# Waiting for freed ring slots in front of every fourth gather, for two groups at once, instead of every second

## The reference

```python
h = relu(layernorm(x))
H = gelu(h @ W1.T + b1)                        # [6250, 128]
X_src = H[src]                                 # [200000, 128]: a gather by edge
W_tar = gelu(X_src @ WA.T) @ WB.T              # [200000, 4]
cross = X_src[:, :, None] * W_tar[:, None, :]
agg = gelu(segment_sum(cross, dst))            # [6250, 128, 4]
out_edge = einsum('ehm,em->eh', agg[dst], W_tar)
agg_node = segment_sum(out_edge, dst) / max(count(dst), 1)
out = x + gelu(concat([agg_node, H])) @ W2.T + b2
```

## Time and profile before

| | |
|---|---|
| median of three runs | 1236.04 us |
| the profiled execution | 1235.48 us |
| its span in the trace | 1233.7 us |
| TensorE (PE) matmul busy | 1053.0 us, 85% |
| VectorE (DVE) busy | 901.9 us, 73% |
| GpSimd (POOL) busy | 851.9 us, 69% |
| ScalarE (ACT) busy | 634.3 us, 51% |
| gathers (L780) | 796, 780.5 us busy |

### The profile page before, as it was taken

The page is one execution under the profiler, slowest core; times in us unless marked ns, Lnnn a source line. Parts: engine busy times, 40 slices in busy tenths (PEclk is TensorE's granted clock), DMA queues, the critical chain, the costliest instruction groups (busy, mean ns, idle before and its releaser), DMA issues.

```text
span 1233.7 us, 26415 instructions
## 1 busy us (share of the span) xinstructions
PE 1053.0 (85%) x7416; PEld 743.9 (60%) x7416; DVE 901.9 (73%) x2876; ACT 634.3 (51%) x1498; POOL 851.9 (69%) x910
## 2 busy tenths in 40 slices
PE   4957776658999998999799899889899989779987
PEld 3744333337778766677576676667676765446644
DVE  8648998884888687898487888668788866263275
ACT  6977766535455465676276667456566540000033
POOL 5437775555777777777777777777777777767445
PEclk9975666668999999999899999989899999889979
DMA  6335554447777755565655556555555667866632
GB/s 217 127 118 177 182 176 158 154 141 218 203 204 213 203 160 155 155 171 166 177 161 160 162 153 169 160 157 165 145 161 161 163 195 213 189 184 186 196 25 88
DMA packets 100422, 205.73 MB, mean 167 GB/s; under 512 B 29570, under 2 KB 48336, under 8 KB 99611
## 3 DMA queue, kind: packets, MB, share of 16 engines
q1 hardware_dynamic: 74804, 146.92, 40.0%
q0 software_dynamic: 25472, 57.11, 18.8%
HBM read 171.73 MB, written 32.22 MB: 165 GB/s over the span
## 4 chain that ended last, share of the span: by engine, by line
PE 42%; DVE 16%; POOL 13%; issue 12%; DMA 8%; ACT 5%; DVEq 3%; SPq 0%; ACTq 0%; POOLq 0%
PE ps L1581 20%; POOL q L780 13%; PE ps L1528 10%; PE ps L1547 7%; DMA q<-node_table,src_g 6%; DVE big L1338 3%; DVE big L1197 3%; PE ps L1531 2%; DVE q L1206 2%; DVE big L1184 2%; DVE mask L1172 2%; PE ps L1586 2%; DVEq L1154 2%; ACT big L823 1%; DMA out_dram<-q 1%
## 5 line engine op out<-in xcount | busy, mean ns | idle before, releaser
L780 POOL DMA_INDIRECT q<-node_table,src_g x796 | 780.5, 981 | 294.6 <-issue 214.4
L1581 PE MATMUL ps<-big,q 128*128 128x298 bf16 (+2 forms) x2940 | 528.9, 301 | 8.2 <-DMA q<-product_parts 7.6
L896 ACT ACTIVATE hot_b<-iota_b,q 128x128 bf16<-128x128 bf16 x848 | 270.0, 389 | 245.4 <-PE ps L1547 245.1
L1528 PE MATMUL ps<-mask,q 128*128 128x96 f32 x1592 | 275.2, 300 | 93.5 <-DVE mask L1172 90.3
L1581 PEld LDWEIGHTS ps<-big,q 128*128 128x128 bf16 x2940 | 267.9, 99 | 110.1 <-DMA q<-product_parts 7.7
L1528 PEld LDWEIGHTS ps<-mask,q 128*128 128x128 f32 x1592 | 236.3, 209 | 147.1 <-DVE mask L1172 133.4
L1206 DVE TENSOR_SCALAR q<-iota_a,q 128x294 bf16<-128x294 f16 (+2 forms) x848 | 238.1, 324 | 38.2 <-issue 22.8
L1547 PE MATMUL ps<-q,hot_b 128*128 128x294 bf16 (+2 forms) x848 | 211.2, 334 | 45.1 <-DVE big L1197 37.6
L1197 DVE TENSOR_TENSOR big<-big,ps 128x294 f32 (+2 forms) x411 | 225.9, 550 | 19.5 <-PE ps L1547 17.9
L1172 DVE TENSOR_TENSOR mask<-eq,q 128x192 f32<-128x192 bf16 x398 | 141.2, 356 | 121.6 <-DMA q<-node_table,src_g 106.0
L1184 DVE TENSOR_TENSOR big<-big,ps 128x120 f32 x398 | 110.1, 277 | 81.1 <-DVE big L1184 42.3
(11 more groups left out here) (145 smaller groups left out, 658.9 us busy)
## 6 DMA issues: line engine op xcount, KB each, us to landing
q<-product_parts SPq DMA_DIRECT2D x245, 388.0 KB
product_parts<-big SPq DMA_DIRECT2D x24, 776.0 KB, 3.5
q<-node_table,src_g POOLq DMA_INDIRECT x796
node_table<-big SPq DMA_DIRECT2D x12, 280.0 KB, 3.1
big<-node_table SPq DMA_DIRECT2D x24, 140.0 KB, 2.2
own_part<-big SPq DMA_DIRECT2D x12, 256.0 KB, 3.2
out_dram<-q SPq DMA_DIRECT2D x12, 256.0 KB, 2.0
big<-own_part SPq DMA_DIRECT2D x2, 1024.0 KB, 6.5
```

The costliest lines, as they stand in the source:

```text
L780: pool.indirect_dma_start(out=ring[:, t % R, :], out_offset=None, in_=table, in_offset=bass.IndirectOffsetOnAxis(ap=src_g[:, t:t + 1], axi ...
L896: last = nc.scalar.activation(hot_b[:, b % 2, i, :], iota_b[:, :], ACT.Abs, bias=nkey_b[:, t:t + 1])
L1528: nc.tensor.matmul(o[:, 0:MIX * W], ring[:, s + t, 0:D], mask[:, b, t, :, :], start=(t == 0), stop=(t == G - 1))
L1581: last = nc.tensor.matmul(ps[:, 3 + m, 0:n], cb[:, LEAD + P * (MIX * part + m):LEAD + P * (MIX * part + m + 1)], counts[k % 2][:, a, c0:c1 ...
```

## The change

```diff
             for t in range(TG):
                 if t == 2:
                     pool.memset(c3[:, :, :, 0:LEAD], 0.0).then_inc(lead_zeroed, 1)
-                if t >= R and t % G == 0:
-                    pool.wait_ge(group_summed, (t - R) // G + 1)
+                if t >= R and t % (2 * G) == 0:
+                    pool.wait_ge(group_summed, min((t - R) // G + 2, NG))
                 pool.indirect_dma_start(
```

## The result

| | before | after |
|---|---|---|
| median | 1235.87 us (8 runs, 1234.14 to 1238.61) | 1245.44 us (8 runs, 1240.49 to 1249.83) |
| ratio | | 1.0080, 95% interval 1.0059 to 1.0101 |
| the profiled execution | 1235.48 us | 1249.71 us |

The change costs 9.6 us, 0.8%. The forecast was 7.9 us slower, 1243.9 us. The profiled execution of the changed kernel is one of its slowest: it lies 14.2 us above that of before, where the medians lie 9.6 apart. So its rows show where lateness comes in, and what the change costs as a whole is taken from the medians of many runs.

The account below looks back on a forecast made before the run. GpSimd's gather stream was taken to bound the kernel from 404 us on; 2.5 + 1.9 + 1.5 + 2.5 - 0.5 = 7.9 us gave a median of 1243.9 us, with a range of +1 to +12.5 us.

Parts of the forecast that it names:

- What bounds the kernel: From 404 us GpSimd issues gathers without a break, 2.5 us a group; lateness stays until something other than the stream decides.
- The waits that go: The 196 waits removed from GpSimd's gathers save 0, since a wait is no instruction of its own; bound 2 us.
- One group later at each place where the ring last held the stream: Where an odd group was last held, the even group takes its release, and everything behind stands 2.5 us later.
- Term 1: Group 86 instead of 87 released at 362.97 us: +2.5 us, bounds 0 and 2.5, on the path from 411.73 us.
- Term 2: Group 300 at 901.34 us must wait for the sum of 295, leaving 1.88 us later: +1.9 us, bounds 0 and 1.9.
- Term 3: Group 368 instead of 369 at 1075.75 us, before `check_bounds`: stream 2.5 us later, taken as +1.5, bounds 0 and 2.5.
- Rival B: Only a part of the slips arrives, TensorE's remaining work absorbing others: +2.5 to +5 us, 1238.5 to 1241; chance 0.22.
- Term 4: Group 380 instead of 381 at 1113.11 us, reaching the end whole over the last landing: +2.5 us, bounds 0.5 and 2.5.
- Stage 0: Group 32 leaves at 188.21 us instead of 33, but its mask starts 16 us later, so the later release costs 0.
- the relief: Entry of stage 1: two tiles fewer gathered while the first `product_parts` load runs, -0.5 us, bounds 0 and -1.5.
- rival D: Faster: at the entry of stage 1 the 5.01 us wait for the first part load mostly goes, 1232 us; chance 0.07.
- The skill's rule: A 72 KB tile lands in 2.2 us, leaving masks some 2 us to spare; the slips shrink to about 1 us, kernel unchanged.

## Why the prediction was right, point by point

**What bounds the kernel.** Right for the middle stretch: in the kernel with the new waits until 404 us a slip of one group was still there 690 us later, 2.6 us. It was incomplete behind it. That the ring was last held at odd groups leaves out the longest hold of all in the last stage, 6.25 us at group 378, and there TensorE's sums take over from the stream. So slips before and behind it don't add up in the stream, only in TensorE's sums.

**The waits that go: 0.** Right within what can be seen. With the waits put back the ratio is 1.0086, against 1.0080.

**One group later at each place where the ring last held the stream.** Right as a mechanism: four counts of tiles at four releases are each two lower. The rings confirm it from the other side. At the same place near 363 us the release went to tile 173 in the changed kernel, 175 before, 177 with 14 slots and 179 with 16.

**Term 1, +2.5 us.** The slip is shown in the stream. What it costs at the end was measured as +1.6 us, with an interval from -0.9 to +4.0, so the 2.5 is neither confirmed nor refuted, and behind group 378 the traces don't tell it from 0. That it is built up after stage 0 and not in it was right.

**Term 2, +1.9 us at group 300 alone: mis-sized.** The changed kernel's trace has six holes there, 5.6 us, and the kernel with the new waits only in that stretch has three, 2.8 us. The step that failed was to take the one trace of before for every execution, and to take only one group from it. At group 300 the new release was late by 1.88 us, but in the same trace it was late by 0.84 us at group 190 (it left at 623.36 us; the sum of group 185 ended at 623.93) and by 0.43 at group 296. At group 206 it was not, but with little to spare: it left at 663.70 us, and the sum of group 201 ended at 663.00, so with the 0.27 us of reaction the margin was 0.4 us. The margin moves by more than that from one execution to the next: the kernel with the waits put back has its holes at 272 and 276 instead, 2.2 us together, and none at 300. So the term is a matter of several places with small margins, 2 to 6 us of holes, of which the time of the middle kernel shows +1.6, from -1.5 to +4.7. I had a sentence for "other even groups may be held in their turn" and left it out of the sum. I had also written that new gaps of more than 3 us there would make the prediction wrong; by that measure this term was wrong in the profiled execution, though the time stayed in the range. Group 300 stands 8.5 us later there and not 4, and the last tile, at 1167.57 us, 13.2 later and not 8; the execution is 14.2 us the slower.

**Term 3, +1.5 us: rather too large, not settled.** From tile 720 on the new waits cost 4.4 us and from tile 752 on 4.3 us, which leaves 0.1 but is known to some 4 us only. In the traces the way from the sum of group 363 to that of group 375 took 37.2 to 38.2 us in the seven kernels with a ring of 12 and the old waits at groups 364 to 375, and 37.9 to 39.5 us in the four with the new ones (the changed kernel 38.3). The stream does stand later in the changed kernel: group 368 waits 3.18 us. The masks before `check_bounds` notice little of it:

```profile
1096.14 0.36 DVE L1172 TENSOR_TENSOR mask<-eq,q 128x192 f32<-128x192 bf16 x1 [2.23 <-DMA q<-node_table,src_g]
...
1097.42 0.36 DVE L1172 TENSOR_TENSOR mask<-eq,q 128x192 f32<-128x192 bf16 x1 [0.93 <-DMA q<-node_table,src_g]
...
1098.79 0.36 DVE L1172 TENSOR_TENSOR mask<-eq,q 128x192 f32<-128x192 bf16 x1 [0.61 <-DMA q<-node_table,src_g]
...
1099.75 0.35 DVE L1235 TENSOR_REDUCE big<-q 1x51 f32<-1x204 int32 x1
```

This is VectorE's timeline going into `check_bounds`. These are the masks of groups 369, 370 and 371. They wait 2.23, 0.93 and 0.61 us, together 3.8, as against 0, 2.10 and 0.94 before, together 3.0: 0.7 us more, although the stream there has slipped by a further group. Rival B and the lower bound seem to describe this place better. That the crowd of other transfers sets these landings fits, but no run takes it away, so it is argued and not shown.

**Term 4, +2.5 us: right place, too small, and not by the path forecast.** The last slip is the largest single part: +4.3 us measured, from +1.7 to +7.0. The traces give it more closely. These are the sums of group 375, which releases group 381 before and 380 after, and of the last group, 397, first before and then after:

```profile
1112.63 0.20 PE L1531 MATMUL ps<-eq,q 128*13 128x24 bf16 x2
1159.92 0.20 PE L1531 MATMUL ps<-eq,q 128*13 128x24 bf16 x2
...
1123.38 0.20 PE L1531 MATMUL ps<-eq,q 128*13 128x24 bf16 x2
1174.12 0.20 PE L1531 MATMUL ps<-eq,q 128*13 128x24 bf16 x2
```

From the one to the other are 47.3 us before and 50.7 after. The six kernels with a ring of 12 and the old waits at this place took 46.9 to 47.6 us, the five in which group 380 waits for group 375 50.7 to 51.9. So the place costs 3.1 to 5.0 us, whichever of these traces are compared. The prediction let the slip reach the end over the last landing. In the changed kernel the chain of waits leaves GpSimd before that, at one late landing, and then runs on TensorE:

```profile
1151.34 0.94 POOL q L780
1152.59 5.79 DMA q<-node_table,src_g
1158.46 0.37 DVE mask L1172
1158.88 0.69 PE ps L1528 x4
```

This is tile 783, of group 391, and TensorE waits for no mask behind it. In all five kernels with the slip the chain leaves at this same tile, with a landing of 5.79 to 6.16 us. Before, the chain went to the last tile, whose landing took 4.45 us. What the late tile meets can be seen on the sync engine's queue, a load of 1,088 KB (L624), first before and then after:

```profile
1142.29 0.37 SPq L624 DMA_DIRECT2D big<-own_part  x1
...
1153.04 0.37 SPq L624 DMA_DIRECT2D big<-own_part  x1
```

A load of `product_parts` (L601, 388 KB) is issued 0.4 us ahead of it in both. Before, the tile issued 0.4 us ahead of L624 was number 785, of group 392; after, it is number 783, of group 391. With the stream one group behind, the late landing falls on a group earlier, and TensorE has one group more to do behind it. That these loads make the landing late fits every trace looked at, but no run moves it, so it is argued and not shown.

**Stage 0 at 0, the relief at -0.5 us.** The first agrees with the traces: GpSimd waits for sums there for 39.5 us instead of 40.0, and the stream's lateness is gone by the release near 363 us. The relief is not shown. At the entry of stage 1 the first load of `product_parts` took 5.01 us before, and 4.55 in the chain after:

```profile
276.64 4.55 DMA q<-product_parts
```

But it began 0.42 us later, so TensorE's first product moved by 0.04 us only. And the load took 4.36 to 4.73 us in six other kernels in which group 56 is issued at its old time, and 4.55 to 5.08 in the four in which it is held. Nothing supports rival D.

**The sum.** The forecast's terms gave +7.9; the changed kernel measures +9.6, with an interval from +7.3 to +12.5. The parts measured alone give 1.6 + 1.6 + 4.4 = 7.6 us, each known to about 3 us. So the total was right within its error, while single terms were off both ways: term 4 too small, term 3 rather too large, the relief absent. That they came out at 7.9 together is in part luck. The size of the middle stretch is open: from the sum of group 81 to that of group 363 took 722.3 us in the changed kernel's trace, 715.8 with the waits put back, and 712.8 before, where kernels with the old waits took 712.1 to 715.3.

**The skill's rule.** By the Trainium skill (DMA: Bandwidth & Descriptors, "Anatomy of one DMA — SWDGE (gpsimd) path") an estimate of 2.2 us for a tile's landing would have left room for the slips and given no change. The trace disagrees: the kernel lost 9.6 us, and landings in the chains took 4.45 and 5.79 us from the start of the issue. The measurement decides against it here.

## What to carry to other kernels

Find the last place where a full buffer held the producer before the producer becomes the bound, and count what was out by then. One group fewer there is one group's time for as long as the producer decides, here over 690 us; it ends where the consumer holds the producer again, so list every such hold, on even and odd groups alike, up to the end. A wait for two groups at once shortens a ring by one group where a full ring decides, and it saved nothing for being fewer waits. Where a margin in one trace is smaller than the scatter between executions, count part of the cost as there already.

## What the runs showed that I had not expected

A total hides much. The stretch from the last sum to the end of the span, which no gather touches, took 73.6 us before and 73.7 after, but 70.6 in the kernel with the new waits in the middle and 77.3 in that with them from tile 720 on. That is as much scatter as the terms that were sought, and the way between two sums shows them more closely. The holes in the middle differ from one profiled execution to another: at groups 150, 206, 230, 296, 300 and 332 in the changed kernel, and at 272 and 276 with the waits put back. Two more groups of ring took 4.4 us off, and VectorE's `hot_a` buffers that gave the room could go from 8 to 6 without a measurable loss (1.0008).
